# Vision tower kernel, graph part: ten products without a reader on TensorE, and batch 1's output moved from GpSimd to VectorE

## What is computed

```python
x = layernorm(h)
n = (x @ W_gat).reshape(M, HEADS, EXPERTS)           # 16 features a node
a_src, a_dst = (n * att_src).sum(-1), (n * att_dst).sum(-1)
e = leaky_relu(a_src[src] + a_dst[dst], 0.2)         # 262144 edges and the self loops
ee = exp(e - segment_max(e, dst)[dst])
agg = segment_sum(n[src] * (ee / segment_sum(ee, dst)[dst])[:, :, None], dst) + b_gat
scores = layernorm_affine(agg).mean over heads       # 4 experts, the best 2 are kept
w = softmax(top2(scores))
out = h + sum_e w_e * (gelu(x @ W1[e] + b1[e]) @ W2[e] + b2[e])
```

## Time and profile before

| | |
|---|---|
| median of three runs | 5094.92 us |
| the three runs | 5090.7, 5094.92, 5100.04 us |
| the profiled execution | 5098.54 us |
| its span, first to last instruction | 5096.9 us |
| granted TensorE clock, mean of the span | 0.922 |
| busy: TensorE (matmul) / VectorE / ScalarE / GpSimd | 86% / 69% / 43% / 19% |
| the graph part | 4633.6 to the end, some 463 us |

### The profile page before, as it was taken

One profiled execution on the slowest core, in us unless ns is written; L12 is line 12 of the kernel. 1 busy time (PEld: TensorE's weight loads), 2 busy tenths in 40 slices (PEclk: granted clock), 3 DMA queues, 4 the chain that ended last, 5 costly groups with the idle time before them and its releaser, 6 DMA issues. The chain is left out here.

```text
span 5096.9 us, 70974 instructions
## 1 busy us (share of the span) xinstructions
PE 4381.6 (86%) x24686; PEld 2709.4 (53%) x24686; DVE 3495.4 (69%) x8785; ACT 2184.4 (43%) x3734; POOL 949.4 (19%) x1116
## 2 busy tenths in 40 slices
PE   7664999999999999999999799999889999995341
PEld 3442444444445454544455355555479988885220
DVE  7656777777777776777755488888755557774444
ACT  1452444444444444444544355555434334332111
POOL 1132111111111111111100000000033330003785
PEclk9887999999999999999999899999879999996555
DMA  2006354656454545565554331110020001000111
GB/s 74 9 25 124 98 143 124 136 120 134 119 147 123 147 119 122 123 134 125 138 133 127 111 96 39 38 27 25 18 51 7 16 7 20 7 6 9 13 19 17
DMA packets 327733, 391.34 MB, mean 77 GB/s; under 512 B 119873, under 2 KB 277837, under 8 KB 326580
## 3 DMA queue, kind: packets, MB, share of 16 engines
q1 hardware_dynamic: 236936, 187.54, 18.5%
q0 software_dynamic: 58368, 172.46, 11.2%
q10 hardware_dynamic: 32076, 26.80, 2.9%
HBM read 313.89 MB, written 70.64 MB: 75 GB/s over the span
## 5 line engine op out<-in xcount | busy, mean ns | idle before, releaser
L1085 PE MATMUL mem_kv<-mem_weights,mem_table 128*128 128x456 f32 x4608 | 1957.3, 546 | 0.0
L1354 DVE SCALAR_TENSOR_TENSOR mem_weights<-mem_above,mem_exps 128x912 f32<-128x912 f32 x1152 | 1273.6, 1106 | 674.8 <-ACT mem_exps L1231 671.8
L1231 ACT ACTIVATE mem_exps<-mem_above 128x912 f32<-128x912 f32 x1152 | 1070.1, 930 | 930.3 <-PE mem_above L1072 930.2
L1085 PEld LDWEIGHTS mem_kv<-mem_weights,mem_table 128*128 128x128 f32 x4608 | 871.7, 189 | 568.0 <-issue 452.0
L1072 PE MATMUL mem_above<-mem_operands,mem_selector 123*128 123x456 bf16 x2304 | 636.7, 357 | 60.7 <-DMA mem_inv_z<-scratch_inv_z 35.5
L2315 DVE TENSOR_REDUCE mha_chunk_max<-mha_max_scores 114x1 f32<-114x342 f32 x864 | 437.6, 513 | 280.0 <-PE mha_max_scores L2083 263.7
L2106 PE MATMUL mha_sums<-mha_probs,mha_value_wide 114*72 114x114 f32 (+1 forms) x5184 | 606.1, 261 | 14.2 <-ACT mha_probs L2297 14.2
L2106 PEld LDWEIGHTS mha_sums<-mha_probs,mha_value_wide 114*72 114x72 f32 (+1 forms) x5184 | 558.1, 143 | 23.2 <-issue 21.0
L1072 PEld LDWEIGHTS mem_above<-mem_operands,mem_selector 123*128 123x128 bf16 x2304 | 223.1, 98 | 568.3 <-issue 500.6
L2297 ACT ACTIVATE mha_probs<-mha_scores 114x912 f32<-114x912 f32 x324 | 297.8, 930 | 382.4 <-PE mha_scores L2095 380.6
L973 POOL DMA_DIRECT2D mem_table<-in_L_ffn_tables_dram x288 | 154.0, 540 | 1352.6 <-PE mem_kv L1085 1347.3
(11 more groups left out here) (607 smaller groups left out, 5052.4 us busy)
## 6 DMA issues: line engine op xcount, KB each, us to landing
mem_table<-in_L_ffn_tables_dram POOLq DMA_DIRECT2D x288, 512.0 KB
mem_operands<-scratch_second_scores SPq DMA_DIRECT2D x216, 256.5 KB
mem_operands<-scratch_first_scores SPq DMA_DIRECT2D x288, 128.2 KB
mem_inv_z<-scratch_inv_z SPq DMA_DIRECT2D x72, 228.0 KB
scratch_second_scores<-mem_sel_parts ACTq DMA_DIRECT2D x81, 171.0 KB
scratch_first_scores<-mem_sel_parts ACTq DMA_DIRECT2D x108, 114.0 KB
scratch_mem_q<-mem_weights SPq DMA_DIRECT2D x16, 513.0 KB, 5.9
scratch_mem_keys<-mem_kvT SPq DMA_DIRECT2D x72, 114.0 KB, 9.1
```

What stands on the lines that cost most here:

```text
L1085: last = nc.tensor.matmul(acc[k][:, 0:SPAN], table[:, k, ch, :], W[:, J % 3, c, :], start=(ch == 0), stop=(ch == CHUNKS - 1))
L1231: nc.scalar.activation(E[:, J % 2, :, :], psD[J % 2][:, :, 0:SPAN], ACT.Exp).then_inc(exped, 1)
L1354: nc.vector.scalar_tensor_tensor(W[:, J % 3, :, :], psD[J % 2][:, :, 0:SPAN], 0.0, E[:, J % 2, :, :], ALU.is_ge, ALU.mult).then_inc(weight ...
```

## The change

Two edits, with no link between them. On TensorE, a helper `keep_busy(n)` issues n f32 matmuls of the 128x128 identity with 342 columns of `xT` (the last batch's, with what an earlier part left there) into `acc_a` and `acc_b` in turns; nothing waits for them and nothing reads them before the projections overwrite them. Eight are issued ahead of the first batch's transposes, two behind them. And the output of batch 1 is formed by VectorE's `combine(1)` right behind `combine(0)`, ahead of the second gates; GpSimd's four operations and its two semaphores go, and SP waits for batch b's sum with `dve_sum >= b + 1`.

```diff
@@ sync
             for b in range(BATCH):
-                if b == 1:
-                    sp.wait_ge(pool_sum, 1)
-                else:
-                    sp.wait_ge(dve_sum, max(b, 1))
+                sp.wait_ge(dve_sum, b + 1)
@@ gpsimd
             for u in range(UNITS):
                 gather(picked[:, u, :], runD, edge.end[:, u:u + 1]).then_inc(picked_in[u // HALF_U], 16)
-            pool.wait_ge(gated, 1)
-            m, rows_h = Y4[:, of(1), :, :], H[:, of(1), :]
-            G.tensor_tensor(m, m, gates[:, :, of(1)].rearrange("p e t -> p t e").unsqueeze(3).to_broadcast([TP, TILES, GE, DIM]),
-                            ALU.mult).then_inc(psum_step, 1)
-            pool.wait_ge(psum_step, 1)
-            G.tensor_tensor(m[:, :, 0:2, :], m[:, :, 0:2, :], m[:, :, 2:4, :], ALU.add).then_inc(psum_step, 1)
-            pool.wait_ge(psum_step, 2)
-            G.tensor_tensor(rows_h, rows_h, m[:, :, 0, :], ALU.add).then_inc(psum_step, 1)
-            pool.wait_ge(psum_step, 3)
-            G.tensor_tensor(rows_h, rows_h, m[:, :, 1, :], ALU.add).then_inc(pool_sum, 1)
@@ tensor
+            def keep_busy(n):
+                for k in range(n):
+                    nc.tensor.matmul(ps_x[k % 2][:, 0:HALF], ident[:, :], xT[:, BATCH - 1, 0:HALF], start=True, stop=True)
+
+            keep_busy(8)
             turn_normed(0)
+            keep_busy(2)
             for b in range(BATCH):
@@ vector
             gates_of(0)
             combine(0)
+            combine(1)
             gates_of(1)
             combine(2)
             combine(3)
```

More of the change, by code:

```diff
@@ L2661, in expert_graph_stage @@
             sem(n) for n in ("norm_step", "centred", "squared", "var_done", "root_done", "normed", "turned", "copied"))
-        wx_step, e_in, up, act_done, down, biased, gated, pool_sum, dve_sum, psum_step, stored = (
-            sem(n) for n in ("w_gat_step", "expert_in", "up", "act_done", "down", "biased", "gated", "pool_summed", "summed_rows",
-                             "pool_step", "out_stored"))
+        wx_step, e_in, up, act_done, down, biased, gated, dve_sum, stored = (
+            sem(n) for n in ("w_gat_step", "expert_in", "up", "act_done", "down", "biased", "gated", "summed_rows", "out_stored"))
         counted, c_turned, n_done, pgated, tgated, dgated = (
```

## The result

The changed kernel took 5080.19 us in the median of 13 runs (5073.27 to 5087.99); the kernel before, run beside it, 5094.92 us. The ratio of the runs is 0.9966, with a 95% interval of 0.9957 to 0.9975: 17.3 us less, between 12.7 and 21.9; the medians lie 14.7 us apart. One of the 13 executions of the kernel before took 6754.22 us, a slow one that the ratio leaves out. The forecast was 5081.4 us.

The account below looks back on a forecast made before the run. TensorE's half-clock transposes and projections, then GpSimd's gathers, were taken as the bound; 8.6 us (products) plus 4.9 (batch 1's output) made 13.5 off the 5094.92 median: 5081.4 us. Range 5079.5 to 5083, widened to 5077 to 5092.

Parts of the forecast that it names:

- The bound: Graph part: the chain enters over TensorE's 18.86 us, then store and gathers; bringing the store forward brings everything behind forward.
- Part one, the products: Norm part, TensorE: unread products raise the clock for three transpose sets and four projections, 10.25 against 18.86 us, 8.6 earlier.
- The clock: TensorE, norm part: granted clock reaches 1.00 before the first transposes and stays up through the projections, instead of 0.50.
- Rival 1: TensorE's clock comes up but falls again within the projections; total gain 7.3 to 9.8 us; chance 0.21.
- Rival 2: TensorE's clock falls before 4643.96 or comes up too late; products give -0.3 to +2 us; chance 0.15.
- Rival 3: TensorE's products do not pipeline and delay the second transposes; slower than before, 5096.6 us; chance 0.03.
- The row at 2995: Profile row, 2995 to 2999: TensorE, 2.81 us of 4 busy, mostly f32 transposes and short products, at 1.00.
- Part two: End of graph part: batch 1's output moves from GpSimd to VectorE; 6.05 less 1.2 gives 4.9 us.
- The cover: VectorE before the second gates: batch 1's four operations fit in its wait for gathers, with 0.8 us left.
- rival 4: All four of batch 1's output operations on VectorE hold the gathers; total gain 10.6 us, 5084.3; chance 0.05.
- So the second gates start 1.2 us later: End of graph part: one gather held 1.17 us by VectorE's operations delays the second gates, to 5056.5.
- The bound of 6.05: Upper bound in us for moving batch 1's output to VectorE, if no gather is held.

Follow-up runs that it names:

- products only: The kernel before with the ten unread TensorE products added and batch 1's output left on GpSimd: 0.9982 of the kernel before, 9.2 us.

## Why the prediction was right, and where it was not

**The bound.** Right. What brought the store forward brought forward all behind it: 9.31 us at the first gather, and products only gained 9.5 in its stage. No new pause came up between the gathers; from the first to the last it took 1.2 us more, 1.0 of them the held one.

**Part one, the products.** Right, with its terms: products 1.15 us apart low and 0.58 high (1.14 and half of it), the clock up 4.36 us from the start (4.3 in the row it was taken from), their end 6.5 us from it (6.7), nothing late. That 4.36 came so near to 4.3 is in part luck: in the six other profiles with fillers ahead of the first transposes it was 3.4 to 4.7 us. And the products did not start at the low level, as was written: the granted clock was still 1.00 for their first 0.9 us. In the chain, transposes took 1.07, 0.91 and 0.89 us (0.95 each), projections 1.73, 1.72, 1.73 and 1.81 (1.85 each), together 9.86 where 10.25 stood. The part gave 8.9 us to the store instead of 8.6, and 0.4 more behind it, where the store landed in 4.21 us instead of 4.60.

**The clock.** The forecast chose that it stays up, and it did, over the whole of the seven pieces. The reason given, no idle time from the second transposes on, fits what the runs show; but the argument gave the work to the wrong products. It was argued that the products ahead of the transposes bring the clock up. They do, but in the one profile with them alone it did not last; the two behind them brought it up and kept it without the eight, and so did one of them in two profiles. Rival 1 did not happen to the change, but it did without its last two products: there the clock fell within the projections and 1.1 us remained. Rival 2 is what 64 rows do. Rival 3 is out by the distance of 1.15 us between products.

The Trainium skill, TensorE: Matmul & The Clock Gate, Part 4, which says that transposes do not count for the full clock as products do, does not hold for these f32 transposes of 128x128: with transposes alone as filler the clock rose 4.69 us from the start and the store came at 20.58 us. The row at 2995 in the earlier trace rows was the better guide.

**Part two.** The contention went as worked out: 7.99 us became 1.78, 6.2 us where 6.05 stood. The cover held (0.88 us of idle time, 0.8 forecast), and one gather was held, as forecast (1.03 us, 1.17 forecast); the last took 1.12 us, so rival 4 is out. **The step that failed is the one after it**: "So the second gates start 1.2 us later". It took the landing to stay 2.50 us behind the last gather's end, though that distance was itself long: the traces have 1.4 to 1.5 us for undisturbed gathers. The runs show in its place a landing that does not move with a gather held by 1.0 us, and a distance that shrinks to 1.45 us. The term of 1.2 us measured 0.0, and part two gave 6.2 us instead of 4.9, just over its upper bound. The bound of 6.05 was the right one for the wrong reason: not that no gather is held, but that it does not matter.

In the Trainium skill, SBUF — State Buffer, Who interferes with whom, a VectorE operation with two SBUF inputs contends with what GpSimd reads, and the section infers that it leaves the writing of descriptors alone. The held gathers (3.41 to 4.65 us against 1.12) speak against it, and the split of such an operation, which gave 10.6 us, says the same by experiment (which of GpSimd's accesses is held, no run shows). What the section says of operations with one SBUF input agrees: the gather that began at 4706.71 under the reduction of 3.75 us took 1.12 us.

**The sum.** 13.5 us forecast, 15.4 by the profile from the start of the graph part: 0.3 too little for the projections, 0.4 for the landing of the store, 1.3 for part two, less 0.1 of other scatter. The median came out 1.2 us under the forecast, within its range; the ratio's interval of 12.7 to 21.9 us holds both sums.

## What to carry to other kernels

When TensorE idles ahead of a stretch on the chain that runs at 0.50, try to fill the last gap before it first, with full-height work (128 rows) that no one reads: here one product of 1.4 us was worth 8.5 to 9 us in two profiles. Look at more than one profile before you trust so little. Where VectorE and GpSimd overlap, ask both ways who holds whom: GpSimd's arithmetic stretched 1.8 us of small VectorE operations to 8, and VectorE's long two-input operations held gathers that GpSimd only issues; moving the one and cutting up the other gave 6 and 11 us. Before a hold is charged, look whether the consumer waits for the issue or for the landing, and what other transfers are under way between the two.

## What was not expected of the hardware

- One f32 product of two records (128x128 by 342 columns, 1.37 us) between nine transposes and nine more took the granted clock from 0.50 to 1.00 for the 10.2 us that followed, after 8.53 us without TensorE work; 31.2 us of nearly unbroken 64-row and thin work did not.
- 64x128 weights in place of 128x128, with the same 342 columns and the same time (1.34 us a product at the low clock), left the clock at 0.50.
- The landing of GpSimd's last gather released the second gates 2.35 to 2.79 us behind the gather's end in four kernels, and 1.45 to 1.52 us in the nine where the gather before it had been held by 1.0 us. The late landings (3.4 to 4.6 us from a gather's start, against 2.5 to 2.7) are those of gathers that met the two busy microseconds of the store of batch 0's output; whether the store causes it was not tested.
- A 72-element VectorE operation took 4.05 us beside a GpSimd operation of 4.11 us.
